# Second cross attention of an eight-layer kernel: projections side by side, scores next to weighing, and one of three bank copies moved to VectorE

## The reference

```python
q = query @ w_q                      # query = layernorm(x), 128 -> 1024
kv = context @ w_kv                  # 96 -> 2048
k, v = jnp.split(kv, 2, axis=-1)
scores = jnp.einsum('bhqd,bhkd->bhqk', q, k) * SCALE
attn = jax.nn.softmax(scores, axis=-1)
out = jnp.einsum('bhqk,bhkd->bhqd', attn, v)
return out @ w_out + b_out
...
x = x + jnp.tanh(g_xattn[3]) * _L3_xattn_ref(_layernorm(x, axis=-1), ctx_768, ...)
```

## Time and profile before

| | |
|---|---|
| median of 3 runs | 2481.77 us (2468.37 to 2483.14) |
| the profiled execution | 2468.89 us |
| its span in the trace | 2467.1 us |
| busy: TensorE, VectorE, ScalarE, GpSimd | 2069.0, 1672.7, 1258.3, 840.0 us |
| the stage that the change touches | about 1906 to 2384 us of the span |

### The profile page before, as it was taken

The page is one execution under the profiler, slowest core; times in us unless marked ns, Lnnn a source line. Parts: engine busy times, 40 slices in busy tenths (PEclk is TensorE's granted clock), DMA queues, the critical chain, the costliest instruction groups (busy, mean ns, idle before and its releaser), DMA issues. The chain is left out here.

```text
span 2467.1 us, 49700 instructions
## 1 busy us (share of the span) xinstructions
PE 2069.0 (84%) x18068; PEld 1574.7 (64%) x18068; DVE 1672.7 (68%) x3302; ACT 1258.3 (51%) x2880; POOL 840.0 (34%) x714
## 2 busy tenths in 40 slices
PE   6668888888887898879999957776698799999964
PEld 3358878787876566646666636665566466666654
DVE  5779999999998888735444355663456566656544
ACT  3278777777772676623322224443143366656631
POOL 1224545444553333234445432221000133323233
PEclk7579999999998899989999967775599899999985
DMA  1100000000000100046344300001000000000001
GB/s 55 40 1 8 13 9 13 8 13 8 13 7 24 57 9 6 2 97 127 69 109 99 70 13 7 7 0 49 0 1 7 4 4 5 5 5 5 1 2 34
DMA packets 41411, 61.71 MB, mean 25 GB/s; under 512 B 9464, under 2 KB 18208, under 8 KB 40800
## 3 DMA queue, kind: packets, MB, share of 16 engines
q1 hardware_dynamic: 41184, 58.66, 9.8%
HBM read 56.02 MB, written 2.62 MB: 24 GB/s over the span
## 5 line engine op out<-in xcount | busy, mean ns | idle before, releaser
L827 POOL TENSOR_TENSOR a_probs<-a_probs,a_rsums 128x1024 f32<-128x1024 f32 x64 | 121.3, 1896 | 322.5 <-DVE a_rsums L875 322.5
L1504 POOL TENSOR_TENSOR f_h<-f_gated,f_w_spread 128x512 f32<-128x512 f32 x128 | 161.6, 1268 | 196.6 <-DVE f_gated L1558 91.7
L1558 DVE TENSOR_TENSOR f_gated<-f_silu,f_up 128x512 f32<-128x512 f32 x128 | 87.1, 686 | 184.3 <-PE f_up L1635 169.8
L2113 POOL TENSOR_TENSOR f_slot_sum<-f_slot_sum,f_logits 128x512 f32<-128x512 f32 x96 | 128.4, 1338 | 214.9 <-ACT f_logits L2298 214.8
L2291 ACT ACTIVATE f_combine<-f_logits,f_neg_row_max 128x128 f32<-128x128 f32 x512 | 198.2, 396 | 0.8 <-DVE f_neg_row_max L2152 0.8
L1598 ACT ACTIVATE f_silu<-f_gate 128x512 f32<-128x512 f32 x128 | 76.2, 597 | 221.1 <-PE f_gate L1635 218.7
L2121 POOL TENSOR_TENSOR f_acc<-f_acc,f_row_factor 128x512 f32<-128x512 f32 x128 | 162.2, 1274 | 4.9 <-DVE f_acc L2187 4.9
L2357 PE MATMUL f_turn_bank<-ident,f_combine 128*128 128x128 f32 x512 | 84.8, 290 | 89.3 <-ACT f_combineT L2279 89.3
L1650 PEld LDWEIGHTS f_acc<-f_down,f_h 128*128 128x128 f32 x1024 | 129.0, 192 | 41.9 <-issue 37.1
L863 DVE TENSOR_REDUCE a_negmax<-a_score_bank 128x8 f32<-128x1024 f32 x64 | 78.2, 1222 | 103.1 <-PE a_score_bank L1004 103.1
L2379 PE MATMUL f_logit_bank<-f_phi,f_xT 128*128 (+1 forms) x1024 | 140.7, 285 | 3.2 <-ACT f_logits L2263 3.1
(11 more groups left out here) (328 smaller groups left out, 5259.1 us busy)
## 6 DMA issues: line engine op xcount, KB each, us to landing
f_w_spread<-f_routing_rows SPq DMA_DIRECT2D x64, 512.0 KB, 10.0
f_w<-in_f_w SPq DMA_DIRECT2D x16, 256.0 KB, 2.5
a_cT<-in_ctxT SPq DMA_DIRECT2D x16, 192.0 KB, 2.5
f_gate_up<-in_f_guT SPq DMA_DIRECT2D x1, 2048.0 KB, 8.2
out<-x_resident SPq DMA_DIRECT2D x8, 256.0 KB, 2.4
c_cT<-in_ctxT SPq DMA_DIRECT2D x8, 192.0 KB, 2.4
a_ctx<-in_ctx SPq DMA_DIRECT2D x8, 192.0 KB, 2.6
f_phi<-in_f_phi SPq DMA_DIRECT2D x1, 1024.0 KB, 5.6
```

The costliest lines, as they stand in the source:

```text
L1504: nc.gpsimd.tensor_tensor(h[:, u % KEPT, :], gated[:, u % 2, :], w_spread[:, u // PER, u % PER, :], ALU.mult).then_inc(weighted, 1)
L2113: nc.gpsimd.tensor_tensor(slot_sum[:, :, :], slot_sum[:, :, :] if g > 1 else raw[:, (m - 1) % RING], raw[:, m % RING], ALU.add).then_inc(p ...
```

## The change

In TensorE's stream the order within a step becomes turn(p+1), projection, projection, mix in even steps, projection, scores(p+3), weigh(p). In VectorE's stream a new `empty` comes first in each step that has a next group: it copies the first of the three projections (number 3p) out of its bank. ScalarE copies the other two, both ahead of the exponential. The one semaphore `emptied` becomes two, `emptied_act` and `emptied_dve`; a projection waits for both with counts worked out in `wait_emptied`. The waits of steps 0, 5 and 6, which make sure that the projections of a group are copied before its scores and weighing read them, move along and count on both. The instructions are the same in number and size; only the copies of 3p change their engine.

```diff
@@ block.vector
+                dve.sem_inc(emptied_dve, PAIRED)
...
+                def empty(at, n):
+                    i, s, it = at
+                    dve.wait_ge(projected, (it - 1) * PROJECTIONS + n + 1)
+                    nc.vector.tensor_copy(projection_out(s, n), project_banks[n % 2][:, :]).then_inc(emptied_dve, 1)
...
                     for p in range(PAIRED):
+                        if after:
+                            empty(after, projections_of(p)[0])
                         pair = pair_at(at, after, p + 2)
                         if pair:
                             total(*pair)
@@ block.scalar
-                act.sem_inc(emptied, 2)
+                act.sem_inc(emptied_act, 2 * PAIRED)
...
                         if after:
-                            for n in projections_of(p)[0:2]:
+                            for n in projections_of(p)[1:]:
                                 empty(after, n)
                         pair = pair_at(at, after, p + 3)
                         if pair:
                             exponentiate(*pair)
                         keep_out(at, p)
-                        if after:
-                            empty(after, projections_of(p)[2])
@@ block.tensor
-                    pe.wait_ge(emptied, (it - 1) * PROJECTIONS + n + 1)
+                    if n >= 2:
+                        wait_emptied(it, n - 1)
+                    else:
+                        wait_emptied(it - 1, PROJECTIONS + n - 1)
                     project(s, n, project_banks[n % 2][:, :]).then_inc(projected, 1)
+
+                def wait_emptied(it, n):
+
+                    pe.wait_ge(emptied_dve, it * PAIRED + (n + 2) // 3)
+                    pe.wait_ge(emptied_act, it * 2 * PAIRED + n - (n + 2) // 3)
...
                             project_ahead(after, mine[0])
-                        if after and p in (5, 6):
-                            pe.wait_ge(emptied, it * PROJECTIONS + (8, 16)[p - 5] + 2)
-                        pair = pair_at(at, after, p + 3)
-                        if pair:
-                            scores(*pair)
-                        if after:
                             project_ahead(after, mine[1])
                         if p == 0 and before:
                             mix(before, G - 1)
@@
                             mix(at, p // 2 - 1)
-                        if p == 0:
-                            pe.wait_ge(emptied, it * PROJECTIONS + 2)
-                        weigh(at, p)
                         if after:
                             project_ahead(after, mine[2])
+                        if after and p in (5, 6):
+                            wait_emptied(it + 1, (8, 16)[p - 5])
+                        pair = pair_at(at, after, p + 3)
+                        if pair:
+                            scores(*pair)
+                        if p == 0:
+                            wait_emptied(it, PROJECTIONS)
+                        weigh(at, p)
```

More of the change, by code:

```diff
@@ L784, in layer6_attention @@
             sem(n) for n in ("start_projected", "start_emptied_by_scalar", "start_emptied_by_vector"))
-        projected, emptied = sem("projected"), sem("emptied")
+        projected, emptied_act, emptied_dve = sem("projected"), sem("emptied_by_scalar"), sem("emptied_by_vector")
         scored, maxed, shifts, exps = sem("scored"), sem("maxed"), sem("shifts"), sem("exps")
@@ L925, in empty @@
                     act.wait_ge(projected, (it - 1) * PROJECTIONS + n + 1)
-                    nc.scalar.activation(projection_out(s, n), project_banks[n % 2][:, :], ACT.Copy).then_inc(emptied, 1)
+                    nc.scalar.activation(projection_out(s, n), project_banks[n % 2][:, :],
+                                         ACT.Copy).then_inc(emptied_act, 1)
                 def exponentiate(at, p):
```

## The result

| | before | after |
|---|---|---|
| median of the timed runs | 2481.84 us (10 runs) | 2497.19 us (10 runs) |
| the profiled execution | 2468.89 us | 2494.01 us |
| its span | 2467.1 us | 2492.2 us |

A forecast was written before the change was run, and what follows sets the result against it. TensorE's queue bounds the kernel before; after, a loop over the softmax chain does. +6.2 us up to the last group and +7.6 in it sum to +13.8, from median 2481.8 to 2495.6, stated as 2495; range 2468 to 2511.

The forecast's parts named there:

- TensorE bounds the kernel now, and the passages cost about 0.10 each: Second cross attention: TensorE's queue is the limit; switching between whole-array and half-array matmuls costs about 0.10 us beside a projection.
- TensorE's own step is 5.72: TensorE's work in a reordered step without a mix: 5.72 us, 0.24 less than 5.96.
- The chain is 8.55: Softmax chain from scores' start through maximum, exponential, sum and normalising to the turn: 8.55 us.
- 5.39 from the turn back to scores: TensorE from turn through two projections, mix and projection to scores: 5.39 us, closing a 13.94 us loop over two steps.
- VectorE's copy costs nothing: VectorE's copy of the first projection ends before the sum's exponential is ready, 0.1 us to spare; costed at nothing.
- The copy of the turned norm, +0.38 per group: ScalarE's copy of the turned norm comes behind the exponential, and step 6's mix waits for it: +0.38 us per group.
- Last group, 12.4 per double step, +7.6 in all: Group without projections: mix waits for ScalarE's copy of weighed values, scores for the mix; 12.4 us per two steps, +7.6.
- rival C: Granted clock falls to its lower level through most of the last group: +18 us, in all +32, 2514; chance 0.07.
- Rivals A and B: A: chain under 7.83, TensorE stays the limit, 2468, chance 0.14. B: VectorE's copy 0.3 us late, 2504, chance 0.13.

The follow-up runs named there:

- early_scores: Kernel before, TensorE's step reordered to turn, scores, weighing, mix, three projections; ScalarE copies all, `keep_out` ahead of the exponential: ratio to before 1.0009, two steps 13.51 us.
- keep_first_short_chain: Changed kernel with `keep_out` ahead of the exponential and GpSimd normalising only 4 of 8 heads: 2465.27 us in a single run, two steps 13.42 us.
- keep_first: Changed kernel with ScalarE's `keep_out` ahead of the exponential instead of behind it: ratio to before 1.0076, two steps 13.90 us.
- old_order_vector_copy: Changed kernel with TensorE's order of before; VectorE still copies the first projection, ahead of its sum: ratio to before 1.0042, two steps 13.95 us.
- mix_after_scores: Changed kernel with TensorE's mix between scores and weighing instead of ahead of the third projection: ratio to before 1.0065, two steps 14.09 to 14.66 us.
- scalar_copies_all: Changed kernel with ScalarE copying all three projections ahead of the exponential and VectorE none: 2590.09 us, two steps 16.09 us and up.
- the shorter chain: Changed kernel with GpSimd normalising only 4 of a pair's 8 heads: ratio to before 1.0099, two steps 14.14 to 14.2 us.
- old_order_sum_first: Changed kernel with TensorE's order of before and VectorE's copy of the first projection behind its sum: ratio to before 0.9978, two steps 13.71 us.

## Why the prediction was right, and where its terms were off

The forecast (2495, within 1% of before) held, and its mechanism did: the passages that TensorE saves are given back through the softmax chain. By its own steps:

- *TensorE bounds the kernel now, and the passages cost about 0.10 each.* Right. early_scores and keep_first_short_chain turn them into 0.20 and 0.29 per two steps, less than the 0.48 that the prediction counted for its own order. Scores to weighing costs nothing extra, 1.09 in after. The Trainium skill, TensorEngine Tiling (Array Packing), Key Properties, counts such a passage as a change of mode that drains the engine; no run here shows it for this one.
- *TensorE's own step is 5.72.* Off: 5.91. The prediction saw the third projection 0.04 late against VectorE's copy and dropped it because the step had slack. It starts 0.95 behind the second instead of 0.86, and the scores start 1.05 behind it instead of 0.95. In after this comes out of the wait at the turn, which is 0.33 to 0.44 in 21 places where 0.6 to 0.8 in 28 was forecast; it costs time where that wait is gone, in keep_first_short_chain.
- *The chain is 8.55.* 8.54.
- *5.39 from the turn back to scores.* This is the term that was mis-sized: 5.61. The prediction let the mix wait for `keep_out` behind the exponential in the last group and did not ask the same in the steady part, where the exponential is later than the place of the mix too. 28 double steps times 0.22 are 6.2 us, nearly all of the 6.6 that the steady part has over its forecast; keep_first takes it away (13.90).
- *VectorE's copy costs nothing.* Right for the sum in after: it starts 4.89 behind its scores, 0.09 behind the end of the copy, so the margin of 0.1 held. But that margin is against one chain only. That the copy ahead of the sum closes a loop of its own, 6.2 us per step, wasn't seen. In after it lies hidden under the longer two-step loop (14.15 against 6.2 + 7.5); without that loop it is the limit, as old_order_vector_copy and mix_after_scores show.
- *The copy of the turned norm, +0.38 per group.* Step 6 takes 8.22 where the other steps with a mix mostly take 7.72 to 7.81, so +0.41 to +0.50.
- *Last group, 12.4 per double step, +7.6 in all.* The loop is right: 38.2 us without the slow mixes, 37.8 forecast. The 3.1 us more are rival C in small: two mixes at the lower clock, where the rival had the whole group and 18 us, and the forecast none. Each time TensorE had waited 1.96 and then 0.87 us shortly before. It is no accident of one profile: scalar_copies_all, whose last group has the same order and the same waits, has both mixes slow too (3.61 and 3.42). The 2.3 us behind the last turn belong here as well; the forecast had nothing there.
- *Rivals A and B* didn't come: two steps are above 13.71 with waits for GpSimd ahead of the turns, and the sum isn't late.

The sum was +13.8. The profile says +25.1, of which +23.9 in the two stretches that the sum covers; the timed runs say about +20. So the terms were too small, all in the same direction. That 2495 lies only 2 us from the measured median is luck in part: the two medians are 15.4 us apart where the ratio of the runs says 20, and the runs of one kernel differ among themselves by about 20 us, more than the whole sum.

## What to carry to other kernels

When instructions move in a hand-ordered stream, look for every loop that the new order closes, over one step and over two, and add up each; a copy or a `keep_out` that is cheap by itself counts by what stands behind it in its queue. A wait that is found in one part of the program (here the mix behind `keep_out` behind the exponential) is to be asked for in all parts. And when an edit opens one loop and the time stays, put it together with the edit that opens the next before dropping either: of 0.7 us per two steps, `keep_out` first gave 0.25 alone and the shorter chain nothing.

## What the runs showed of the hardware

- One branch back of the loop over groups cost 2.1 us in before and 6.0 in early_scores. TensorE stands 1.76 to 2.33 us there in the three kernels with the old order of its stream, and 2.60 to 3.14 in the seven with another order (2.68 in after).
- Waits of 2 to 3 us are often followed by the lower clock, but not always. Behind the branch the granted clock was lower in six of those seven kernels (after 2.60 us in mix_after_scores, 2.73 in keep_first, 2.98 in early_scores) and stayed at 1.00 in after, after 2.68. In scalar_copies_all it fell after 1.86. In the last group of after it fell after 1.96 and 0.87 about 1 us apart, and stayed at 1.00 after a wait of 1.70 (2358.91). A wait of 1.89 us in the same place of the last group was followed by 1.00 in before (2364.08) and by 0.74 in old_order_sum_first (2381.20). What decides between them stays open.
- A mix whose weight load waits for a semaphore takes 1.89 to the next start, one that doesn't 1.78.
- Matmuls on half the rows followed by such on half the columns cost nothing extra (1.09); to or from the whole array it is about 0.10.
